# A graph network on one core: the counts of a block stored in four transfers instead of one

## The reference

```python
def _L0_gnn_ref(x, e, conv_W, conv_b, att_W, ...):      # four layers
    ...
        a = jnp.exp(jax.nn.leaky_relu(logit, negative_slope=0.2))
        n = jax.ops.segment_sum(a, dst, num_segments=n_nodes)
        h = jax.nn.relu(x / jnp.where(n == 0.0, 1.0, n))
        x = _rmsnorm(h + x, nw, nb)
        y = jax.nn.relu(x @ hW.T + hb)
        x = _rmsnorm(x + y, hnw, hnb)
def _L1_gnn_ref(nfeat, src, dst, etype, ...):           # softmax over the edges of a node
    ...
    out = jax.ops.segment_sum(a[:, None] * nfeat[src], dst, num_segments=n)
def _L2_gnn_ref(x, edge_index, ...):                    # two graph convolutions
    def _graph_conv(h, src, dst, n, W_root, W_rel, b):
        agg = jax.ops.segment_sum(h[src], dst, num_segments=n)
        return h @ W_root.T + agg @ W_rel.T + b
    ...
def _L3_gnn_ref(x, edge_index, edge_weights):
    messages = x[src] * edge_weights[:, None]
    out = jax.ops.segment_sum(messages, tgt, num_segments=x.shape[0])
x = _layernorm(x + _L0_gnn_ref(...)); x = _layernorm(x + _L1_gnn_ref(...))
x = _layernorm(x + _L2_gnn_ref(...)); x = _layernorm(x + _L3_gnn_ref(...))
```

## Time and profile before

| | us |
|---|---|
| median of three runs | 5016.61 |
| the profiled execution | 5045.92 |
| its span, from the first to the last instruction | 5044.1 |
| `weighted_sum(0)` (the stage with the stores), about | 1745 to 3108 |
| first and last store of counts issued | 1761.8 and 3092.0 |
| the two graph convolutions, loads of the counts from and to | 3141.6 and 3901.7 |
| TensorE busy in the span | 3952.9 (78%) |
| VectorE, ScalarE, GpSimd busy | 3501.3, 2096.5, 833.0 |

### The profile page before, as it was taken

One profiled execution on the slowest core, in us unless ns is written; L12 is line 12 of the kernel. 1 busy time (PEld: TensorE's weight loads), 2 busy tenths in 40 slices (PEclk: granted clock), 3 DMA queues, 4 the chain that ended last, 5 costly groups with the idle time before them and its releaser, 6 DMA issues.

```text
span 5044.1 us, 235969 instructions
## 1 busy us (share of the span) xinstructions
PE 3952.9 (78%) x108221; PEld 3198.5 (63%) x108221; DVE 3501.3 (69%) x4156; ACT 2096.5 (42%) x2474; POOL 833.0 (17%) x760
## 2 busy tenths in 40 slices
PE   5533958769275188888888886999899799999997
PEld 4532847669275166666666654898799566666665
DVE  5876667867757466666666666553455499999997
ACT  5101011020100166766666764664466144544553
POOL 0665757442440400000000000000000000000000
PEclk8975877859577599999999998998899599999998
DMA  6741543526143211111111111553455000000000
GB/s 160 236 136 31 143 138 86 145 73 182 26 118 117 56 54 48 56 49 52 54 52 54 53 54 49 170 178 118 134 178 173 2 10 11 11 10 10 11 11 17
DMA packets 220740, 411.43 MB, mean 82 GB/s; under 512 B 114530, under 2 KB 138980, under 8 KB 219988
## 3 DMA queue, kind: packets, MB, share of 16 engines
q1 hardware_dynamic: 195960, 389.52, 24.8%
q0 software_dynamic: 23904, 10.76, 1.1%
q10 hardware_dynamic: 184, 0.08, 0.0%
HBM read 291.44 MB, written 112.84 MB: 80 GB/s over the span
## 4 chain that ended last, share of the span: by engine, by line
PE 68%; DVE 10%; issue 8%; POOL 5%; ACT 3%; DMA 1%; SPq 0%; DVEq 0%; ACTq 0%; POOLq 0%
PE psum L1122 19%; PE psum L1094 14%; PE psum L1152 12%; PE psum L917 9%; PE psum L1082 4%; POOL heads_d L615 2%; PE psum L885 1%; POOL gath L623 1%; POOL space L629 1%; PE psum L873 1%; DVE space L1659 1%; ACT space L762 1%; PE psum L998 1%; PE psum L999 1%; PE psum L859 1%
## 5 line engine op out<-in xcount | busy, mean ns | idle before, releaser
L767 ACT COPY space<-psum 128x784 f32<-128x784 f32 x1184 | 966.2, 816 | 646.2 <-PE psum L1094 645.1
L1094 PE MATMUL psum<-space 64*128 64x49 bf16 x56832 | 987.5, 184 | 197.5 <-issue 168.5
L1094 PEld LDWEIGHTS psum<-space 64*128 64x128 bf16 x56832 | 853.2, 94 | 405.6 <-issue 297.0
L1122 PE MATMUL psum<-space,X 128*64 128x256 f32 x7252 | 1040.5, 398 | 14.8 <-issue 11.9
L1659 DVE TENSOR_TENSOR space<-space 128x2352 bf16<-128x2352 bf16 x592 | 814.9, 1376 | 0.0
L917 PE MATMUL psum<-table,space 128*128 128x56 bf16 x24300 | 678.5, 189 | 120.2 <-DVE space L1295 76.5
L917 PEld LDWEIGHTS psum<-table,space 128*128 128x128 fp8e4 x24300 | 664.2, 96 | 134.5 <-issue 119.4
L1655 DVE TENSOR_TENSOR space<-space,V 128x2048 bf16<-128x2048 bf16 x592 | 721.4, 1219 | 0.0
L1654 DVE TENSOR_TENSOR space<-space,V 128x784 bf16<-128x784 bf16 x592 | 335.3, 566 | 475.0 <-PE psum L1094 458.6
L762 ACT CAST space<-psum 128x784 uint8<-128x784 f32 x592 | 482.9, 816 | 404.0 <-PE psum L1082 402.0
L1152 PE MATMUL psum<-space 128*128 128x192 bf16 x7252 | 628.3, 247 | 23.9 <-DVE space L1734 23.9
(11 more groups left out here) (276 smaller groups left out, 2698.7 us busy)
## 6 DMA issues: line engine op xcount, KB each, us to landing
space<-adj_d SPq DMA_DIRECT2D x148, 784.0 KB, 4.3
space<-onehots SPq DMA_DIRECT2D x240, 432.0 KB
adj_d<-space SPq DMA_DIRECT2D x74, 784.0 KB, 3.6
onehots<-space SPq DMA_DIRECT2D x60, 432.0 KB, 3.5
space<-digit_rows SPq DMA_DIRECT2D x60, 378.0 KB
space<-cw_d SPq DMA_DIRECT2D x74, 160.0 KB, 3.3
cw_d<-space SPq DMA_DIRECT2D x4, 1184.0 KB, 13.2
heads_d<-spread,heads_at POOLq DMA_INDIRECT x280
```

The lines of the kernel that those rows point to most:

```text
L767: nc.scalar.copy(A[:, h, :, b * P:(b + 1) * P].rearrange("p a (w s) -> p w a s", w=2)[:, :, :, c:c + UC], psum[:, 2 + 2 * (k % 2):4 + 2 * ...
L1094: mm = nc.tensor.matmul(psum[:, 2 + 2 * (k % 2) + w, c * NB:(c + 1) * NB], ohlo[lo:hi, ring, col // 2, :, col % 2], ohw[lo:hi, ring, r, co ...
L1122: mm = nc.tensor.matmul(pb[6][half:half + F, 0:2 * P], X[:, a, :], A[:, 1 - h, a, :], start=(a < 2), stop=(a >= NB - 2))
```

## The change

A block is stored in four transfers of 13, 12, 12 and 12 of the 49 columns (rows of 1664 or 1536 bytes) instead of one. The first waits as before for the block's eighth unit, the second for one unit more, the third for two and the fourth for three, so they are issued while the next block is being made. In the last block of all, the four follow one another at once. The load of the next codes stands between the stores of the two blocks of a pair, and no longer after both. `adj_stored` now counts to 64 for a block.

```diff
--- before.py
+++ after.py
@@ -65,6 +65,7 @@
 HS = P // HC
 PART = 4
 EVERY = PART // 4
+STORES = [(0, 13), (13, 25), (25, 37), (37, NB)]
 MIXED = (NB - 1) // PART * EVERY + 1
 NWT = -(-NDB // 4)
 NOROW = 100.0
@@ -519,19 +520,27 @@
                 for h in range(2):
                     sp.dma_start(cw[:, h, :], cw_d[n, h]).then_inc(cw_loaded[h], 16)
 
+            def store_counts(i, h, b, last=False):
+
+                for q, (lo, hi) in enumerate(STORES):
+                    sp.wait_ge(adj_made, i * (4 * GU) + ((2 * h + b + 1) * GU + (0 if last else q)))
+                    sp.sem_inc(sp_ok, 1)
+                    at = slice(4 * i + 2 * h + b, 4 * i + 2 * h + b + 1) if isinstance(i, int) else bass.ds(i * 4 + (2 * h + b), 1)
+                    sp.dma_start(adj_d[at, :, lo * P:hi * P].rearrange("b p x -> (b p) x"),
+                                 adj[:, b, lo:hi, :].rearrange("p a s -> p (a s)")).then_inc(adj_stored[b], 16)
+
             def pair(n, i, h, more=True):
 
                 if n == 0:
-                    for b in range(2):
-                        sp.wait_ge(adj_made, i * (4 * GU) + (2 * h + b + 1) * GU)
-                        sp.sem_inc(sp_ok, 1)
-                        at = slice(4 * i + 2 * h + b, 4 * i + 2 * h + b + 1) if isinstance(i, int) else bass.ds(i * 4 + (2 * h + b), 1)
-                        sp.dma_start(adj_d[at].rearrange("b p x -> (b p) x"), adj[:, b, :, :].rearrange("p a s -> p (a s)")).then_inc(adj_stored[b], 16)
+                    store_counts(i, h, 0)
                 if more:
                     sp.wait_ge(hot_ready, i * (2 * HS) + (n * NDB * HS + (h + 1) * HS))
                     sp.sem_inc(sp_ok, 1)
                     at = slice(2 * i + h + 2, 2 * i + h + 3) if isinstance(i, int) else bass.ds(i * 2 + (h + 2), 1)
                     sp.dma_start(cw[:, h, :], cw_d[n, at].rearrange("d p x -> (d p) x")).then_inc(cw_loaded[h], 16)
+
+                if n == 0:
+                    store_counts(i, h, 1, isinstance(i, int) and 2 * i + h == NDB - 1)
 
             def pairs(n):
 
@@ -550,7 +559,7 @@
 
                 for h in range(2):
                     if n == 0:
-                        sp.wait_ge(adj_stored[h], 16 * NDB)
+                        sp.wait_ge(adj_stored[h], 16 * len(STORES) * NDB)
                         sp.wait_ge(summed, NDB)
                     else:
                         sp.wait_ge(cast_act, NRB)
@@ -655,7 +664,7 @@
             pool.wait_ge(scan_stored, 16 * (LAYERS + 1))
             gather_chunks(wrow, scans_d.rearrange("(c e) a -> c (e a)", e=KC), KC)
             for h in range(2):
-                pool.wait_ge(adj_stored[h], 16 * NDB)
+                pool.wait_ge(adj_stored[h], 16 * len(STORES) * NDB)
             pool.wait_ge(summed, NDB)
             nc.gpsimd.memset(xT[F:F + 1, :], 1.0).then_inc(ones_back, 1)
 
@@ -757,7 +766,7 @@
                         u = i * (4 * GU) + (n * NDB * 2 * GU + h * 2 * GU + k + 1)
                         if n == 0:
                             if k % GU == 0 and not (fixed and i == 0 and h == 0):
-                                act.wait_ge(adj_stored[b], i * 32 + 16 * h)
+                                act.wait_ge(adj_stored[b], i * (32 * len(STORES)) + 16 * len(STORES) * h)
                             act.wait_ge(adj_psum, u)
                             nc.scalar.copy(adj[:, b, :, :].rearrange("p a (w s) -> p w a s", w=2)[:, :, :, c:c + UC],
                                            psum[:, 0:2, 0:UC * NB].rearrange("p w (s a) -> p w a s", a=NB)).then_inc(adj_made, 1)
@@ -806,7 +815,7 @@
             for n in range(2):
                 if n == 0:
                     for h in range(2):
-                        act.wait_ge(adj_stored[h], 16 * NDB)
+                        act.wait_ge(adj_stored[h], 16 * len(STORES) * NDB)
                 copy_xt(0, NB)
                 for r in range(4):
                     block_step(n, 0, r, r)
```

## The result

| | before | after |
|---|---|---|
| median (runs) | 5017.05 us (4) | 4971.32 us (4) |
| lowest to highest | 5010.98 to 5024.88 | 4965.77 to 4978.11 |
| the profiled execution's span | 5044.1 | 4968.9 |
| first to last copy of counts (the stage) | 1343.6 us | 1272.9 us |

The ratio is 0.9909 (95% interval 0.989 to 0.9927): 46 us faster, where 45 were forecast. The two profiles show 75 us between them, and 71 of these lie in the stage with the stores.

A forecast was written before the change was run, and what follows sets the result against it. TensorE, starved of instruction pages by stores, was taken to bound the stage; - 65.5 - 9 + 27 + 2 = - 45 us took the profiled 5045.9 to 5001, the median to 4971. Range 4935 to 5025, the forecast's own 4956 to 4992.

The forecast's parts named there:

- The bound and the cause: Stage with the stores: TensorE sets the pace; a store holds back its 16 KB instruction pages until done.
- What the stores cost: TensorE in the stage: 65.5 us of idles after stores plus 9 us of low clock, 74.5 us in all.
- the 8 us put down to chance: TensorE idles 2 to 6 us after a store: 8 of 73.5 us expected anyway at the later phase's rate.
- the whole step: Whole kernel: profiled execution from 5045.9 to 5001 us; the same step from the 5016.6 median gives 4971.
- What the parts cost: TensorE in the stage: 27 us of stalls from four parts of 0.7 us, plus 2 us from the codes' load.
- rival 1: Stage's stores: parts hardly hold pages, TensorE's stock covers 0.36 us, all 74.5 us gained, 4942 us; chance 0.15.
- The codes' load: Sync queue between a pair's blocks: goes out some 4 us earlier; by itself 5 pages, 2 us of stalls.
- The added waits: Sync queue and ScalarE's buffer: later parts cost nothing, with 7 us of cover; at the end at most 1 us.
- The low clock: TensorE after long idles: spells at 1.2 GHz costing 9 us, which go as idles over 2 us do.
- Rival 3: Stage's stores: each part holds pages as long as a whole store, so slower by 25 us, 5041; chance 0.14.
- Rival 2: Stage: no change, as stores only accompany the idles or other waits take over; 5017 to 5005 us; chance 0.18.

The follow-up runs named there:

- hardly any store: Changed kernel, but one column of 49 stored per block and only two whole blocks stored at the stage's end for the third stage: 4972.75 us against 5031.62, ratio 0.9892.
- the second profile: The kernel before, unchanged, profiled once more: stage 1320.0 us, 130.6 us of idles of 0.6 us and more.

## Why the prediction was right

**The bound and the cause** held. TensorE sets the pace, and a store keeps its instructions away. Three runs show it: with hardly any store 54 us go, stores added where nothing waits for them bring such idles, and parts in their place bring few. That the idles are waits for pages is shown by where they lie, a whole number of pages apart.

**What the stores cost** was mis-sized: 65.5 us of idles and 9 us of low clock, 74.5 in all, where the version with hardly any store measures 54. For that one execution the sum was nearly right: its stage is 72 us longer than the one with hardly any store. But the execution was heavy: against the 96.9 us of idles of the version with hardly any store its 154.6 us leave 58 us, and the second profile's 130.6 leave 34. Within the sum, the 8 us put down to chance were too few, since with hardly any store the same 4 us hold 16.5 us of idles. The prediction had seen that its execution lay 29 us above the median, and carried the whole step over to the median all the same. That is the step that failed. (A count over the trace gives 4 pages where the prediction has 3, and 57 where it has 55, which changes nothing.)

**What the parts cost** was mis-sized the other way: 27 + 2 us of new stalls, where by their ratios the changed kernel and hardly any store differ by 3 to 9 us, and in the idles by nothing that can be seen. Two things were off. A part holds the engines for 0.56 us and not for 0.7, near the bound by bytes and not by the rows of the codes' load. And the delay was turned into stalls nearly in proportion, while two, four and seven parts show that small delays bring hardly any. So what rival 1 said of the parts is what happened; its price of 75 us was wrong, as it took the same 74.5.

Both errors were of 20 to 26 us and of opposite sign, so the time of 4971 us is right to the microsecond by luck. What the working had earned is its own range of 4956 to 4992.

**The codes' load** had no term for its move; the prediction put the longest idles down to it. Alone it gives 11 us.

**The added waits** cost nothing, as said: no wait of ScalarE for a store is in the profile after, and seven parts, whose last goes out six units late, are no slower than four.

**The low clock "goes, as idles over 2 us do"** was too simple. In the profile of before 32 groups of eight products at line 1122 take over 1.2 us, in the second 25; in the three profiles after 20 to 22 still do, though no idle is over 1.7 us, and with hardly any store 21. Nor is its price of 9 us confirmed. TensorE's busy time in the stage is 1144, 1140 and 1139 us in the three profiles of before, 1131, 1136 and 1136 in those after and 1130 with hardly any store; but it is 1150 with only the codes moved and 1139 and 1147 with seven parts, so it differs as much between executions.

**Rival 3**, a hold as long for a part as for a whole, falls with the gain and with the seven parts. **Rival 2** falls with the ratio. The rule of the Trainium skill ("Runtime: NRT & Kernel Launch", "Instruction fetch mechanics") that crossings of 16 KiB blocks are mostly hidden does not describe this stage: 54 us go with the stores, and some 90 us of idles at the borders of pages stay without them. The Trainium skill's rule to coalesce small transfers ("DMA: Bandwidth & Descriptors", "Rules for kernel authors") is right about the engines' own time, 2.2 us for a block in four parts against 2.0, and here that time was not what counted.

What stays open is why pages come too late for 90 us of idles that the stage keeps with 10 GB/s of traffic. Their place says that they are waits for pages too, but no run here changed how pages are fetched or how fast TensorE uses them up.

## What to carry to other kernels

Where TensorE's program is written out, its instructions are themselves a stream of transfers: look for idles in mid-row with no releaser, see whether they lie a fixed number of instructions apart (here 256), and set them beside the large transfers in order of time. A large store that nobody waits for may be cut in two to four parts, a unit of work apart; its own duration is not the price, its length in one piece is. And before carrying a step from one profile to the median, take a second profile, above all when the first lies beside the median: here 24 us of the stage were that execution's own.

## What the runs showed of the hardware

- A transfer of 784 KB keeps pages of instructions out for its 2.0 us (2 pages in 74 stretches of 1.5 us); four transfers of 192 or 208 KB, issued 0.57 to 0.60 us apart, let them in (0.36 per us).
- TensorE's idles of 0.6 us and more without a releaser lie at the borders of pages, multiples of 256 instructions apart: all 99 steps with hardly any store, all 129 before, all 90 after. They end 2.1 us or more after the start of the last page.
- 128 rows of 1664 bytes from the core to memory take the engines 0.56 us, 71 ns a row; of 6272 bytes 2.0 us, 243 ns a row.
- 518 transfers in place of 296, on a queue with time to spare, cost nothing that the runs could tell (0.9897 and 0.9898 of the time before).
